# Attention and experts on one core: where the queue of SyncE loads the stacked rows of batches 2 and 3

## The reference, cut to what matters

```python
q = split_heads(x @ Wq + bq); k = split_heads(x @ Wk + bk); v = split_heads(x @ Wv + bv)
scores = jnp.einsum('bhqd,bhkd->bhqk', q, k) / math.sqrt(hd)
scores = jnp.where(causal[None, None], scores, -10000.0)
ctx = jnp.einsum('bhqk,bhkd->bhqd', jax.nn.softmax(scores, axis=-1), v)
...
x = _layernorm(x + attn(x)); x = _layernorm(x + xattn(x, ctx)); x = _layernorm(x + ffn(x))
```

## Time and profile before

| | us |
|---|---|
| median of 3 runs | 705.12 |
| the three runs | 697.10, 705.12, 707.01 |
| the profiled execution | 699.31 |
| its span, first to last instruction | 697.6 |
| mean granted TensorE clock, as a share | 0.954 |

### The profile page before, as it was taken

How to read it: one execution, slowest core, us unless ns; L and a number is a source line. 1 busy time by engine, 2 the same in 40 slices (tenths; PEclk the granted TensorE clock), 3 DMA queues, 4 the chain that set the end, 5 groups by cost and what they waited for, 6 DMA issues and landing times. The chain is left out here.

```text
span 697.6 us, 13600 instructions
## 1 busy us (share of the span) xinstructions
PE 609.1 (87%) x5242; PEld 416.8 (60%) x5242; DVE 529.3 (76%) x929; ACT 407.8 (58%) x622; POOL 306.1 (44%) x362
## 2 busy tenths in 40 slices
...
GB/s 226 144 0 151 92 153 151 92 219 176 1 1 61 137 108 1 61 34 59 2 32 91 0 2 226 168 280 269 272 277 295 262 266 299 261 283 224 87 224 165
DMA packets 69648, 102.07 MB, mean 146 GB/s; under 512 B 5040, under 2 KB 55432, under 8 KB 68560
## 3 DMA queue, kind: packets, MB, share of 16 engines
...
...
## 5 line engine op out<-in xcount | busy, mean ns | idle before, releaser
L238 DVE TENSOR_REDUCE rowmax<-M 128x1 f32<-128x512 f32 (+3 forms) x176 | 104.6, 636 | 44.1 <-PE M L228 42.1
L683 ACT ACTIVATE probs<-R 128x1024 f32<-128x1024 f32 x80 | 80.4, 1027 | 57.8 <-PE R L1037 57.4
L211 PE MATMUL HB<-xT,w 128*128 128x256 f16 (+1 forms) x1104 | 106.4, 256 | 0.0
L1758 PE MATMUL YB<-w,h 128*128 128x256 f16 x936 | 105.9, 273 | 0.1
L211 PEld LDWEIGHTS HB<-xT,w 128*128 128x128 f16 x1104 | 94.4, 98 | 9.7 <-DVE xT L1603 0.9
L1758 PEld LDWEIGHTS YB<-w,h 128*128 128x128 f16 x936 | 91.5, 98 | 10.7 <-issue 0.4
L545 POOL TENSOR_SCALAR_AFFINE_SELECT probs<-probs 128x256 f32<-128x256 f32 x128 | 49.7, 408 | 102.2 <-ACT probs L683 101.4
L1463 ACT ACTIVATE hf<-HB,b 128x256 f32<-128x256 f32 (+1 forms) x184 | 69.8, 445 | 35.2 <-PE HB L211 32.3
...
L1378 POOL DMA_INDIRECT xg<-scratch_xs,src x39 | 64.6, 1657 | 26.7 <-PE XB L1745 10.9
L1615 DVE SCALAR_TENSOR_TENSOR w<-w2f,w 128x2048 f16<-128x2048 f32 x23 | 52.7, 2290 | 8.7 <-ACT w L1449 8.7
L1630 DVE SCALAR_TENSOR_TENSOR h<-hf,h 128x512 f16<-128x512 f32 (+1 forms) x92 | 56.3, 612 | 3.2
...
## 6 DMA issues: line engine op xcount, KB each, us to landing
w1f<-in_W SPq DMA_DIRECT2D x23, 1024.0 KB
w2f<-in_W SPq DMA_DIRECT2D x23, 1024.0 KB
scratch_ax<-stage SPq DMA_DIRECT2D x16, 256.0 KB, 2.5
scratch_vw<-stage SPq DMA_DIRECT2D x16, 256.0 KB, 2.8
vw<-scratch_vw SPq DMA_DIRECT2D x4, 1024.0 KB, 5.7
a_x<-scratch_ax SPq DMA_DIRECT2D x4, 1024.0 KB, 6.4
parts<-scratch_ys SPq DMA_DIRECT2D x8, 512.0 KB, 7.5
scratch_qk<-qk SPq DMA_DIRECT2D x6, 512.0 KB, 3.9
```

The lines of the kernel that those rows point to most:

```text
L211: last = nc.tensor.matmul(out, left(a, k), right(b, k), start=(k == 0 and m == 0), stop=(k == n - 1 and m == 2))
L238: return nc.vector.tensor_reduce(rowmax[:, t, par * PAIRS + p0:par * PAIRS + p0 + pairs], bank[:, 0:pairs * wide].rearrange("p (n w) -> p ...
L683: A.activation(probs[:, n % RING, :, :], bank[:, :, :], ACT.Exp, scale=1.0 / (QS * QS)).then_inc(empty, 1)
L1758: last = M.matmul(YB[q][:, t, :], h[:, q, a, m, t * 128:t * 128 + 128], w2[:, q, b, m, :], start=((m, a, b) == (0, 0, 0)), stop=((m, a) == ...
```

## The change

Two steps are moved in ORDER, and with them the DMAs that they issue on SP; no other engine has a part in them. `stack:2`, which stood behind `o.d:0:0`, now stands directly behind `max:1`, and so ahead of `A.s:7` and `VW.s:7`. `stack:3`, which stood behind `o.d:1:1`, now stands ahead of `max:2`. The rest of the diff is the same words broken into other lines.

```diff
-VW:6:0 s:0:17 VW.l:6:0 VW.s:6:0 m:1:21 pv:0:2 s:0:18 store:2:0 A:7:0 ct:0:2 w:0:9 mT:1:0 max:1:0 A.l:7:0 ct.n:0:2
-cx.l:0:0 cx:0:1 s:1:2 cx.l:0:1 idle:243:7 o:0:0 o.d:0:0 stack:2:0 r:0:0 s:1:3 o:0:1 o.d:0:1 m:2:0 r:0:1 vw:0:0 w:1:0
-cx:1:0 max:2:0 cx.l:1:0 O:0:3 cx:1:1 O.d:0:3 r:0:3 cx.l:1:1 v:3:0 o:1:0 n:0:3 s:2:0 o.d:1:0 r:1:0 o:1:1 s:2:1 o.d:1:1
-stack:3:0 r:1:1 m:3:0 ax:1:0 s:2:2 n:1:0 s:2:3 m:3:1 w:2:0 n:1:1 x1b:1:0 s:2:4 m:3:2 w:2:1 m:3:3 xa:1:0 xa.l:1:0
...
+m:1:21 pv:0:2 s:0:18 store:2:0 A:7:0 ct:0:2 w:0:9 mT:1:0 max:1:0 stack:2:0 A.l:7:0 ct.n:0:2 A.s:7:0 s:0:19 w:0:10
+cx.l:0:1 idle:243:7 o:0:0 o.d:0:0 r:0:0 s:1:3 o:0:1 o.d:0:1 m:2:0 r:0:1 vw:0:0 w:1:0 ax:0:0 n:0:0 s:1:4 m:2:1 n:0:1
+w:1:10 m:2:21 T:0:6 w:1:11 T.l:0:6 pv:1:3 T:0:7 mT:2:0 T.l:0:7 ct:1:3 ct.n:1:3 n:0:2 cx:1:0 stack:3:0 max:2:0 cx.l:1:0
```

More of the change, by code:

```diff
@@ L109 @@
 xT:0:0 xT.l:0:0 xT:0:1 x_in:1:0 wh:0:0 xT.l:0:1 wh:0:1 wh:1:0 wh:1:1 q:0:0 q:0:1 idle:256:14 wk:0:0 ql:0:0 idle:226:3
[L110 to L118, removed]
@@ L119 @@
-m:1:14 s:0:12 w:0:5 s:0:13 xr_in:0:0 VW.s:4:0 m:1:15 A:5:0 A.l:5:0 pv:0:1 m:1:16 q:2:1 m:1:17 ql:2:1 A.s:5:0 VW:5:0
-m:1:18 ct:0:1 VW.l:5:0 w:0:6 s:0:14 VW.s:5:0 s:0:15 A:6:0 ct.n:0:1 m:1:19 m:1:20 A.l:6:0 A.s:6:0 w:0:7 s:0:16 w:0:8
-VW:6:0 s:0:17 VW.l:6:0 VW.s:6:0 m:1:21 pv:0:2 s:0:18 store:2:0 A:7:0 ct:0:2 w:0:9 mT:1:0 max:1:0 A.l:7:0 ct.n:0:2
-A.s:7:0 s:0:19 w:0:10 VW:7:0 VW.l:7:0 v:2:0 VW.s:7:0 w:0:11 pv:0:3 wg.l:0:0 s:1:0 xb:0:0 s:1:1 ct:0:3 ct.n:0:3 cx:0:0
-cx.l:0:0 cx:0:1 s:1:2 cx.l:0:1 idle:243:7 o:0:0 o.d:0:0 stack:2:0 r:0:0 s:1:3 o:0:1 o.d:0:1 m:2:0 r:0:1 vw:0:0 w:1:0
@@ L124 @@
[L124 to L128, removed]
@@ L129 @@
-s:1:13 O.d:0:1 T:0:4 r:0:2 w:1:6 s:1:14 ct.n:1:1 s:1:15 T.l:0:4 m:2:14 w:1:7 m:2:15 T:0:5 w:1:8 ql:3:0 pv:1:2 T.l:0:5
-s:1:16 m:2:16 S.p:0:3 q:3:1 m:2:17 ct:1:2 ct.n:1:2 m:2:18 xe:0:3 ql:3:1 s:1:17 w:1:9 xs:0:3 m:2:19 s:1:18 O:0:2 xp:0:3
-s:1:19 O.d:0:2 m:2:20 store:3:0 w:1:10 m:2:21 T:0:6 w:1:11 T.l:0:6 pv:1:3 T:0:7 mT:2:0 T.l:0:7 ct:1:3 ct.n:1:3 n:0:2
-cx:1:0 max:2:0 cx.l:1:0 O:0:3 cx:1:1 O.d:0:3 r:0:3 cx.l:1:1 v:3:0 o:1:0 n:0:3 s:2:0 o.d:1:0 r:1:0 o:1:1 s:2:1 o.d:1:1
-stack:3:0 r:1:1 m:3:0 ax:1:0 s:2:2 n:1:0 s:2:3 m:3:1 w:2:0 n:1:1 x1b:1:0 s:2:4 m:3:2 w:2:1 m:3:3 xa:1:0 xa.l:1:0
@@ L134 @@
[L134 to L153, removed]
@@ L154 @@
-r:3:2 T:3:4 T.l:3:4 T:3:5 T.l:3:5 idle:221:3 xe:3:3 xs:3:3 n:3:2 O:3:2 tp:0:0 tp:1:0 idle:228:3 O.d:3:2 xp:3:3 T:3:6 T.l:3:6 T:3:7
-T.l:3:7 O:3:3 tp:2:0 tp:3:0 tp:4:0 tp:5:0 O.d:3:3 r:3:3 n:3:3
+ql:0:1 cT:0:0 cT.l:0:0 wk.l:0:0 st:0:0 idle:224:3 m:0:6 st:0:1 m:0:14 st:0:2 m:0:2 v:0:0 wk:1:0 m:0:7 idle:225:3 m:0:15
+xT:1:0 xT.l:1:0 st:0:3 m:0:8 st:0:4 m:0:16 xT:1:1 st:0:5 st:0:6 xT.l:1:1 va:0:0 m:0:0 m:0:3 st:0:7 m:0:9 wk.l:1:0 q:1:0
+m:0:17 m:0:10 cT:1:0 m:0:18 W:0:0 cT.l:1:0 wk:2:0 m:0:4 m:0:11 W.l:0:0 ql:1:0 q:1:1 wk.l:2:0 m:0:19 W:1:0 m:0:12 m:0:20
@@ new lines @@
+ql:1:1 kv:0:0 W.l:1:0 m:0:1 kv.l:0:0 wo:0:0 kv:1:0 m:0:5 kv.l:1:0 v:1:0 m:0:13 A:0:0 kv:2:0 A.l:0:0 wo.l:0:0 store:1:0
+m:0:21 x_in:2:0 stack:1:0 A.s:0:0 kv.l:2:0 kv:3:0 mT:0:0 max:0:0 kv.l:3:0 VW:0:0 VW.l:0:0 VW.s:0:0 A:1:0 A.l:1:0 m:1:0
+s:0:0 s:0:1 xT:2:0 A.s:1:0 m:1:1 s:0:2 VW:1:0 va:1:0 xT.l:2:0 xT:2:1 VW.l:1:0 s:0:3 w:0:0 VW.s:1:0 xT.l:2:1 x_in:3:0
+m:1:2 A:2:0 A.l:2:0 A.s:2:0 s:0:4 m:1:3 m:1:4 s:0:5 w:0:1 m:1:5 s:0:6 VW:2:0 m:1:6 VW.l:2:0 w:0:2 pv:0:0 VW.s:2:0 A:3:0
+m:1:7 m:1:8 ct:0:0 A.l:3:0 wg:0:0 w:0:3 s:0:7 ct.n:0:0 s:0:8 m:1:9 s:0:9 A.s:3:0 m:1:10 s:0:10 m:1:11 VW:3:0 VW.l:3:0
@@ new lines @@
+VW.s:3:0 m:1:12 A:4:0 A.l:4:0 w:0:4 s:0:11 A.s:4:0 VW:4:0 VW.l:4:0 q:2:0 ql:2:0 m:1:13 m:1:14 s:0:12 w:0:5 s:0:13
+xr_in:0:0 VW.s:4:0 m:1:15 A:5:0 A.l:5:0 pv:0:1 m:1:16 q:2:1 m:1:17 ql:2:1 A.s:5:0 VW:5:0 m:1:18 ct:0:1 VW.l:5:0 w:0:6
+s:0:14 VW.s:5:0 s:0:15 A:6:0 ct.n:0:1 m:1:19 m:1:20 A.l:6:0 A.s:6:0 w:0:7 s:0:16 w:0:8 VW:6:0 s:0:17 VW.l:6:0 VW.s:6:0
+m:1:21 pv:0:2 s:0:18 store:2:0 A:7:0 ct:0:2 w:0:9 mT:1:0 max:1:0 stack:2:0 A.l:7:0 ct.n:0:2 A.s:7:0 s:0:19 w:0:10
+VW:7:0 VW.l:7:0 v:2:0 VW.s:7:0 w:0:11 pv:0:3 wg.l:0:0 s:1:0 xb:0:0 s:1:1 ct:0:3 ct.n:0:3 cx:0:0 cx.l:0:0 cx:0:1 s:1:2
@@ new lines @@
+cx.l:0:1 idle:243:7 o:0:0 o.d:0:0 r:0:0 s:1:3 o:0:1 o.d:0:1 m:2:0 r:0:1 vw:0:0 w:1:0 ax:0:0 n:0:0 s:1:4 m:2:1 n:0:1
+x1b:0:0 w:1:1 m:2:2 xa:0:0 xa.l:0:0 xa:0:1 va:2:0 xa.l:0:1 w:1:2 m:2:3 S:0:0 S.d:0:0 S:0:1 pv:1:0 s:1:5 S.d:0:1 s:1:6
+xe:0:0 m:2:4 ct:1:0 ct.n:1:0 m:2:5 s:1:7 m:2:6 xT:3:0 S:0:2 xs:0:0 S.d:0:2 xT.l:3:0 w:1:3 S:0:3 S.d:0:3 xp:0:0 T:0:0
+xr_in:1:0 T.l:0:0 T:0:1 T.l:0:1 xe:0:1 s:1:8 S:0:4 xs:0:1 S.d:0:4 S:0:5 O:0:0 S.d:0:5 xp:0:1 O.d:0:0 S:0:6 m:2:7 w:1:4
+S.c:0:6 xe:0:2 m:2:8 s:1:9 S:0:7 m:2:9 S.c:0:7 s:1:10 m:2:10 T:0:2 xT:3:1 T.l:0:2 xT.l:3:1 T:0:3 w:1:5 s:1:11 T.l:0:3
```

27 lines of the change are left out of this document (added).

## The result

| us | before | after |
|---|---|---|
| median, lowest to highest, 20 runs each | 702.35 (697.10 to 708.01) | 708.16 (702.83 to 717.64) |
| ratio, 95% interval | | 1.009 (1.0065 to 1.0115) |
| profiled execution | 699.31 | 704.85 |
| its span | 697.6 | 703.1 |

The change costs 0.9%: 6.3 us by the ratio (4.6 to 8.1), 5.5 us between the two profiled spans. It is clear of noise and well inside 2%.

The account below looks back on a forecast made before the run. TensorE, busy 87% of the span, was taken to bound the kernel, standing still at batch ends for stacked rows. +5.4 us (batch 0) less 3.2 (batch 1), +2.2, on the median 705.12 gave 707, range 698 to 713.

Parts of the forecast that it names:

- End of batch 0, the loads: stack:2 starts at 145.6 instead of 148.97, rows land at about 157.8; taken alone 3.4 us of gain.
- End of batch 0, the stores: Last four stores, behind the loads, land at about 159.9; ACT and o:0:0 wait, xa:0:0 comes 5.4 us later.
- the lower bound: End of batch 0: last store lands at 157.7, about 2.9 us after its issue with nothing ahead of it.
- the value taken: End of batch 0: stores stand behind the rows in the DMA engines and land at about 159.9.
- The clock behind it: After 8 us of standstill, half clock adds 1.25 us to o:0's first group, 1.0 to its second; 0.9 taken back later.
- End of batch 1: s:2:0 waits 1.2 us for the maxima, m:3:0 starts 2.9 us sooner without waiting, xa:1:0 3.2 us sooner.
- the prediction's upper bound: End of batch 1: the maxima land 3.7 us after their issue, at 239.4, as if each were one of the rows.
- The rival of the late maxima: End of batch 1: maxima so late at s:2:0 that the clock falls; +6.7 us in all, 712; chance 0.17.
- The better bound of this place: End of batch 1: largest gain, 4.3 us, with the maxima landing at 237.2 and costing nothing.
- The sum's lower bound: Both batch ends at their bounds: 3.2 us lost less 4.3 us gained, -1.1 us.
- The early loads pay: Rival: both TensorE waits at the batch ends go and nothing replaces them; 10.1 us gained, 695; chance 0.06.
- The sum: Both batch ends together: +5.4 - 3.2 = +2.2 us, 0.3%, all else as it was.

Follow-up runs that it names:

- e6: Changed kernel with each stack:2 load bringing one of eight pairs of heads; no time given, ACT's first ctxT 16.3 us after mT:1.
- e1: Kernel before with only stack:2 moved ahead of the last stores: 708.37 us against 700.18, ratio 1.0104.
- e3: The changed kernel run again as it stands, against the kernel before: 707.55 us, ratio 1.0125.
- e2: Kernel before with only stack:3 moved ahead of max:2: 698.77 us, ratio 0.9973.
- e4: Kernel before with loads moved early but woven: three of stack:2 ahead of VW.s:7, five of stack:3 ahead of max:2; 698.48 us, ratio 0.9958.
- e9: Kernel before with woven early loads, two ahead of VW.s:7, and short fills of unread matmuls ahead of m:2:0 and m:3:0: 697.00 us, ratio 0.9896.
- e8: Changed kernel with unread matmuls, 43 instead of 7 ahead of o:0:0 and 8 ahead of s:2:0: 703.06 us, ratio to before 0.9982.

## Why the prediction came out as it did

The direction was right and the time, 708.16, lies in the range; the size was too small: +2.2 us forecast, +6.3 measured (4.6 to 8.1).

- *End of batch 0, the loads.* Twelve loads ahead of the stores, SP held for 7.7 us: it was 8.2 us (147.92 to 156.12). The wait at `m:2:0` vanished, as expected.
- *End of batch 0, the stores.* The stores land behind the rows and ACT waits for them: right, and the size too. ACT was to start 8.2 us later than now (151.73 to 159.9); from `mT:1` it was 8.8. The 1.9 us for bytes in e6 are the step between the lower bound and the value taken, 2.2 us; the 2.9 us estimated for a store with nothing ahead of it were 3.1 there.
- *The clock behind it.* The first group of `o:0` took 2.72 us, as taken from the earlier trace rows; the second 1.48 and not 2.5, as TensorE was back at full clock by then. That made `m:2:0` come 4.6 us after `o:0:0` where I had 5.5, and from there to `xa:0:0` it took 5.7 us (169.75 to 175.45) for 6.1. These two, both too large, outweigh ACT's start, which was 0.6 too small. `xa:0:0` came 4.7 us later (e1 4.4, e3 5.6; 5.5 from the means) against 5.4.
- *End of batch 1.* `s:2:0` waited 1.87 us (e2 1.36, e3 1.65) for 1.2 forecast. It started 3.7 us after the issue of the maxima had ended (247.52 less 243.77; e2 3.4, e3 3.7), which is the prediction's upper bound and not the 2.7 us it took. The clock stayed at 1.00, `m:3:0` waited for nothing, and the place gave 3.2 us (e2 3.7, e3 3.4): the term of the forecast. The rival of the late maxima did not occur. The better bound of this place, 4.3, was set too low: without a late `s:2:0` there is no 0.6 us for a late norm to take off, and 4.1 + 0.9 are 5.0, as e4 has it. The sum's lower bound is then -1.8, not -1.1.
- *The early loads pay*: excluded by e1, in which the wait for the stores took the place of the wait for the rows. The advice of the Trainium skill ("DMA: Bandwidth & Descriptors", "Rules for kernel authors") to issue early holds in e4 and e9, where nothing urgent stands behind all the loads, and not in the change.
- *The sum.* This is the step that was mis-sized. +5.4 - 3.2 came out as +4.7 - 3.2 in the trace, or +1.7 from the means, but the time moved by 6.3. I had taken it that both stretches start from drained engines and that nothing else in the program feels the change, and I had put the clock's share at 1.4 us lost at the end of batch 0 (2.3 added, 0.9 taken back), 0.9 saved at the end of batch 1, and nothing elsewhere. With the longer standstill filled, no loss against before can be measured (e8), and the runs of e3 have a mean granted clock 0.006 lower than those of before, worth about 4 us by the estimate above. Both make TensorE's clock the likely cause of the surplus, but they do not prove it, and the traces do not show where it sits. They show how much can hide elsewhere: the other pieces differ by up to 1.6 us (between), 3.1 us (to `mT:3`) and 3.7 us (`mT:3` to the end) over the thirteen profiles, and by 0.2, 1.5 and 3.6 us among the three of before. One such piece in the kernel after is the stretch at 186 to 188 above, at half clock with a full TensorE, in a piece 1.2 us longer than before.
- *The median.* I set 707 on a median of 705.12 of three runs; with twenty it is 702.35. A forecast of the ratio would have been 1.003 where it is 1.009, so the time looks better hit than it was.

What stays open is where the remaining 4 us of the change are lost, and whether it is the clock that loses them. One profile of each kernel cannot tell, when the pieces that have no edit in them vary by as much; it would take a dozen profiled executions of both.
